# Layer 0's attention: one subtract on VectorE and one exponential of 512 columns in place of eight of 64

## The reference, cut to what matters

```python
scores = jnp.einsum('bhqd,bhkd->bhqk', Qm, Km) / jnp.sqrt(jnp.float32(Dh))
scores = jnp.where(attn_mask[:, None, :, :], scores, fill)
attn = jax.nn.softmax(scores, axis=-1)      # over 64 context tokens
A = jnp.einsum('bhqk,bhkd->bhqd', attn, Vm)
```

## Time and profile before

| what | value |
|---|---|
| median of 3 runs | 2477.66 us (2474.67 to 2482.07) |
| profiled execution, its own time | 2481.42 us |
| span of its profile | 2479.3 us |
| busy: TensorE, VectorE, ScalarE, GpSimd | 2241.2, 1453.5, 1420.2, 794.9 us |
| exponentials of the attentions (L1248) | 2048 instructions, 485.5 us of ScalarE |
| warm matmuls (L1031) | 1728 instructions, 450.1 us of TensorE |

### The profile page before, as it was taken

How to read it: one execution, slowest core, us unless ns; L and a number is a source line. 1 busy time by engine, 2 the same in 40 slices (tenths; PEclk the granted TensorE clock), 3 DMA queues, 4 the chain that set the end, 5 groups by cost and what they waited for, 6 DMA issues and landing times.

```text
span 2479.3 us, 42343 instructions
## 1 busy us (share of the span) xinstructions
PE 2241.2 (90%) x11319; PEld 1477.3 (60%) x11319; DVE 1453.5 (59%) x5504; ACT 1420.2 (57%) x5145; POOL 794.9 (32%) x870
## 2 busy tenths in 40 slices
PE   6979999999999989899999989898888988797987
PEld 3655756556565656566575747465655656575654
DVE  6554576676665657565676766575654646363621
ACT  2634658567484837474665757484664654665722
POOL 2121111201222222222133222223544444574655
PEclk9999999999999999999999999998999999888989
DMA  6030200100303030202021111204333332544323
GB/s 184 28 108 16 62 18 15 49 1 16 93 10 82 1 86 6 75 26 74 26 60 41 50 52 29 80 13 137 103 86 114 99 116 76 158 138 115 91 60 103
DMA packets 237206, 167.09 MB, mean 67 GB/s; under 512 B 97105, under 2 KB 230575, under 8 KB 236990
## 3 DMA queue, kind: packets, MB, share of 16 engines
q1 hardware_dynamic: 222654, 139.51, 20.1%
q0 software_dynamic: 14336, 25.28, 3.5%
HBM read 123.86 MB, written 53.40 MB: 71 GB/s over the span
## 4 chain that ended last, share of the span: by engine, by line
PE 51%; issue 14%; DVE 14%; ACT 8%; POOL 6%; SPq 4%; DMA 2%; DVEq 0%; POOLq 0%; another core or an unknown queue 0%; ACTq 0%
PE p L1055 8%; PE p L1014 6%; PE p L1031 6%; PE p L989 6%; PE p L952 4%; PE p L1003 4%; PE p L963 3%; PE p L946 3%; ACT l_scratch L1248 3%; PE pg L1023 2%; DVE ln_stats L1463 2%; PE p L1112 2%; SPq L788 2%; PE p L986 1%; DVE l_xres L1493 1%
## 5 line engine op out<-in xcount | busy, mean ns | idle before, releaser
L1248 ACT ACTIVATE l_scratch<-p,l_mx 128x64 f32<-128x64 f32 x2048 | 485.5, 324 | 37.2 <-DVE l_mx L1510 25.2
L1031 PE MATMUL p<-warm 128*128 128x512 bf16 x1728 | 450.1, 393 | 0.0
L1816 POOL TENSOR_TENSOR ln_rstd<-ln_ve,neghalf 128x4 f32<-128x4 f32 x96 | 98.4, 1025 | 731.6 <-DVE ln_ve L1472 730.4
L1023 PEld LDWEIGHTS pg<-slots,wcat 128*128 128x128 f32 x1024 | 175.2, 196 | 233.6 <-DVE slots L1764 161.1
L1014 PEld LDWEIGHTS p<-l_vg,l_scratch 128*128 128x128 f32 x2048 | 256.6, 194 | 60.8 <-ACT l_scratch L1256 33.3
L1031 PEld LDWEIGHTS p<-warm 128*128 128x128 bf16 x1728 | 177.5, 107 | 163.7 <-issue 35.3
L1014 PE MATMUL p<-l_vg,l_scratch 128*128 128x34 f32 x2048 | 262.3, 275 | 5.4 <-ACT l_scratch L1256 2.7
L1832 POOL TENSOR_TENSOR l_scratch<-l_scratch,gp 128x512 f32<-128x512 f32 x128 | 162.3, 1270 | 322.4 <-DVE l_sums L1515 321.4
L989 PE MATMUL p<-l_kbd,l_qT 128*128 128x512 f32 x512 | 262.8, 595 | 0.0
L1023 PE MATMUL pg<-slots,wcat 128*128 128x16 f32 x1024 | 178.3, 250 | 75.4 <-DVE slots L1764 54.9
L1510 DVE TENSOR_REDUCE l_mx<-p 128x8 f32<-128x512 f32 x256 | 176.4, 690 | 99.3 <-PE p L989 90.6
(11 more groups left out here) (302 smaller groups left out, 4120.1 us busy)
## 6 DMA issues: line engine op xcount, KB each, us to landing
xln<-xln_dram SPq DMA_DIRECT2D x40, 512.0 KB, 3.8
x_dram<-l_xres SPq DMA_DIRECT2D x32, 512.0 KB, 4.1
l_vg<-v_dram SPq DMA_DIRECT2D x30, 544.0 KB
l_kbd<-k_dram SPq DMA_DIRECT2D x512, 16.0 KB
xln_dram<-l_xnat SPq DMA_DIRECT2D x16, 512.0 KB, 3.0
l_xres<-x_dram SPq DMA_DIRECT2D x16, 512.0 KB
x_dram<-l_xnat SPq DMA_DIRECT2D x16, 512.0 KB
xin<-in_x SPq DMA_DIRECT2D x12, 512.0 KB, 3.7
```

The costliest lines, as they stand in the source:

```text
L1023: pe.matmul(pg[:, 0:B], wcat[:, :], slots[:, s % STEPS, :], start=True, stop=True).then_inc(l_pe, 1)
L1031: pe.matmul(banks[1][0] if layer > NC_ else px, warm[:, 0:P], warm[:, :], start=True, stop=True)
L1248: i = act.activation(w.ex[b % 2][:, NE * j + h, :], banks[lane][j][:, h * SK:(h + 1) * SK], ACT.Exp, scale=-1.0, bias=w.mx[:, u % 4, h:h + 1])
```

## The change

In layer 0 alone, the planner's four exp steps of a block become two: a new step `apart` on VectorE, and one exp step on ScalarE. `apart` waits for the minimum and for pturn u-4, subtracts each head's minimum from its 64 columns with one instruction of 512 columns (the minimum is read with a stride of zero along a head), and writes the difference from PSUM to `w.ex`. ScalarE then takes exp(-x) of those 512 columns in place, SBUF to SBUF, with no bias operand. Score u waits for `apart` of block u-2 and no longer for its exp. The semaphore `top` now tells that `apart` is done in layer 0 (in layer 1, as before, that the minimum is); the minimum in layer 0 and the sum in layer 1 share a renamed semaphore `reduced`.

```diff
     for u in range(2 * GB):
         steps += [
-            ("pe", "score", u, 1.1, [("qland", u % 2), ("neg", 0), ("exp", 4 * (u - 2) + 3)]),
+            ("pe", "score", u, 1.1, [("qland", u % 2), ("neg", 0), ("exp", 4 * (u - 2) + 3) if l else ("apart", u - 2)]),
             ("dve", "max", u, 0.65, [("score", u), ("exp", 4 * (u - 4) + 3)])]
-        steps += [("act", "exp", 4 * u + e, 0.45, [("max", u), ("pturn", u - 4)])
-                  for e in range(4)]
+        if l == 0:
+            steps += [("dve", "apart", u, 0.7, [("max", u), ("pturn", u - 4)]), ("act", "exp", 4 * u + 3, 0.62, [("apart", u)])]
+        else:
+            steps += [("act", "exp", 4 * u + e, 0.45, [("max", u), ("pturn", u - 4)]) for e in range(4)]
...
                 if family == "score":
                     if u < 2:
                         pe.wait_ge(t.lands, 4 * m + u + 1)
+                    elif layer == 0:
+                        pe.wait_ge(t.top, N - 1)
                     else:
                         pe.wait_ge(t.exped, N - 1)
...
                     (b, j), N = divmod(u, 2), 2 * GB * m + u
+                    if layer == 0:
+                        act.wait_ge(t.top, N + 1)
+                        part = w.ex[b % 2][:, NE * j:NE * j + NE, :]
+                        act.activation(part, part, ACT.Exp, scale=-1.0).then_inc(t.exped, 1)
+                        return
...
-                    dve.tensor_reduce(w.mx[:, u % 4, :], banks[l][j].rearrange("p (a k) -> p a k", a=NE), AX_X, ALU.min).then_inc(t.top, 1)
+                    dve.tensor_reduce(w.mx[:, u % 4, :], banks[l][j].rearrange("p (a k) -> p a k", a=NE), AX_X, ALU.min
+                                      ).then_inc(t.top if layer else t.reduced, 1)
+                elif family == "apart":
+                    dve.wait_ge(t.reduced, N + 1)
+                    if u >= 4:
+                        dve.wait_ge(t.turned, N - 3)
+                    dve.tensor_tensor(w.ex[b % 2][:, heads, :], banks[l][j].rearrange("p (a k) -> p a k", a=NE),
+                                      w.mx[:, u % 4, :].rearrange("p (a o) -> p a o", o=1).broadcast_to([P, NE, SK]),
+                                      ALU.subtract).then_inc(t.top, 1)
```

10 lines of the change are left out of this document (5 added, 5 removed).

## The result

The changed kernel takes 2469.04 us (median of 20 runs, 2456.92 to 2478.64), the kernel before 2477.57 us in the same comparison (20 runs). The ratio is 0.9962, 95% interval 0.9947 to 0.9977: faster by 8.5 to 9.4 us, where I had forecast 20. The time lies in the forecast range, but less than half of the gain came, and the first rival's 2475 us is nearer to it than my 2458.

What follows compares the result with a forecast made beforehand. It took TensorE to bound stage 0, the recurrent network stage 1, and ScalarE's exponentials part of stage 2's attention. Terms -1 + 5 - 24 = -20 us gave 2458 us from the median 2477.66; range 2447 to 2470, chance 0.50.

Steps and rivals of the forecast that it cites:

- the first rival: All attention: TensorE is the bound everywhere and filler was never in the way, so 2475 us; chance 0.18.
- Unit costs: Layer 0's blocks: new exponential 0.62 us, subtract 0.69; ScalarE's busy time falls about 164 us, VectorE's rises 88.
- Stage 0, -1: Stage 0's two bodies: TensorE is the bound with 1.5 us to give, so 1 us off for both.
- Stage 1, +5: Stage 1's two bodies: recurrent steps wait longer behind running long instructions, 0.08 us a step, 5 us slower for both.
- Stage 3, 3 us a body: Stage 3's bodies: relieved ScalarE lets attention shrink until TensorE is the bound, saving 3 us each.
- Stage 2, 3 us a body: Stage 2's bodies: exponentials bound part of attention; relieving ScalarE saves 3 us each, with VectorE staying below the bound.
- The slower one: Subtracts on VectorE delay stage 1's recurrence, 5.5 us a body, and stages 2 and 3, 0.5: 2493 us; chance 0.12.
- ScalarE as the bound everywhere: All attention windows: ScalarE, not TensorE, was at its bound, so stages 0, 2 and 3 shrink to 2417 us; chance 0.06.
- The Trainium skill's rule of weight loads: Weight-load busy time, not matmul time, measures TensorE, making ScalarE the bound in stage 0 as well: 2417 us.
- The fourth: As the forecast, plus norms and projections filling TensorE's gaps outside attention, 4 us more a body in four bodies: 2442 us; 0.14.

Runs made afterwards that it cites:

- half1: The changed kernel with stage 1's subtract and exponential each in two halves of 256 columns: 2478.82 us, ratio 0.9957 to the kernel before.
- No1: The changed kernel with stage 1 put back to eight exponentials of 64 columns: 2466.52 us, ratio 0.9928 to the kernel before.
- whole: Against the kernel before, layer 0 takes one 512-column exponential straight from PSUM, minimum taken but unused, no subtract: 2456.63 us, ratio 0.9885.
- the runs with the fill: The changed kernel, or it with stage 1 put back, plus 14 warm matmuls in stage 2's first body: ratios 0.9989 and 0.9895 to the kernel before.
- nomin: Against the kernel before, one 512-column exponential straight from PSUM in all four stages, neither minimum nor subtract in layer 0: 2439.20 us, ratio 0.9799.
- no1_fill: The changed kernel with stage 1 as before the change and 14 more warm matmuls in stage 2's first body: 2445.98 us, ratio 0.9895.

## Where the forecast was right and where it was wrong

- **Unit costs.** Right: 0.625 and 0.687 us a piece for 0.62 and 0.69. The busy times moved by 76 and 141 us for 88 and 164, by overlap for the most part.
- **Stage 0, -1.** Right in that the stage hardly moved (311.4 and 312.0 against 310.9 to 313.2), with TensorE at 35.00 of 35 us and the chain through it alone; a gain of 1 us can't be told from that spread.
- **Stage 1, +5.** The waits that I priced were about right, and the term was short by what I left out: +8 to +9. A step waits behind an instruction that runs, and half1 shows that its length counts. I had taken 32 steps with two crossings of 0.05 us behind subtracts, 3.2 us a body, and 3.6 were measured; behind exponentials I had 3.2 before and 2.6 after, and it was 3.8 and 1.2. Put together that is 1.0 us a body where I had 2.6. But each of the second body's 64 steps is 7.7 / 63 = 0.12 us longer, since in the new order they also fell behind minima, divisions and norms. For a new order I had no term, as if all else stood where it was. No1 has stage 1 back at 330.2 us. Its ratio of 0.9928 against 0.9962 prices more than stage 1: its ways into stage 2's repeats are 9.2 us shorter than in after.
- **Stage 3, 3 us a body.** Right: 3.4 in the repeated bodies. Some of it went into the ways between them (7.6 and 11.7 us before, 10.6 and 12.6 after, with a spread of 1 to 2 us in before itself), and the stage gave about 11 us for 12.
- **Stage 2, 3 us a body.** This is the step that failed. I wrote that "VectorE at 25.81 + 5.5 = 31 of 40 us stays below it" and let the subtract cost nothing. The long exponential alone brought 5.1 us a body, even more than I took. The subtract took back 3.7, so 1.4 were left. A busy share of 80% in the window was no reason for a price of nothing. It failed in a second way too: I took what the attentions give for what the body gives. They gave 3.9 us, but in the new order they start 6.7 us later, and only 4.1 of that came back behind them. Lane 1's chain, which goes through VectorE twice a block (minimum and sum) and through GpSimd, looks like the cause, and the traces don't bear it out: in the third body lane 1's sums reach over 46.9 us before, 39.0 in after and 36.9 in whole, so this chain is shorter after the change and at most 2 us longer by the subtract. Which wait makes the subtract cost 3.7 us stays open. To that came, in the first body, 6 to 7 us from the lower clock in 6 of 7 profiles, for which I had no term. The filler whose going I had counted as gain is what the runs with the fill put back, and with it TensorE had no second stretch at 1.2 GHz in that body.
- **The rivals.** TensorE at its bound everywhere (2475) is out: nomin goes on to 0.9799 with TensorE's work unchanged. The slower one is right in that the subtract costs as much as it says, 19 us over all stages against its 15, but in other places: 4 to 4.4 us a body of stage 1 for its 5.5, with the exponential in it, and 3.7 a body of stage 2 for its 0.5; and it left out the exponential's gain of 29. ScalarE as the bound everywhere (2417) is out as well, since 14 us less of ScalarE in stage 0's window left the stage as long as it was and its chain on TensorE. The Trainium skill's rule of weight loads, by which that rival went (Perfetto Trace Analysis, Identifying the Most-Contended Engine), isn't borne out there: TensorE is what the chain runs through, with 26.08 of 35 us of weight loads before, beside ScalarE's 31.53. The fourth, with 4 us more a body of stage 3 from outside attention, is out: the stage gave 11 us, and what stands outside its attentions grew by 2.7 us a body.
- **What stays open.** Stages 0 to 3 of the profiles make 1699.8 us before (mean of three) and 1695.6 after (mean of two), 4 of the 9 us measured. The rest would have to lie in stages 4 to 6, whose lengths differ by more than that between chips. The profiles are single executions, and the 20 runs on each side that give 9 us have no stages to compare.

The fastest kernel with the subtraction kept is no1_fill, the change without stage 1 and with the fill: 2445.98 us, ratio 0.9895. It beats both kernels, measured beside before and, on the same chip, the changed kernel (0.9967, 0.9949 to 0.9984).

## What to carry to other kernels

When work moves from a full engine to one that is 65% busy, price it twice: once alone, by a run that only adds it, and once as what stands ahead of the other chains on that engine. The question is not only whether the engine has room, but who waits behind the new instruction, and for a recurrence of short steps the length of one instruction counts. Where a planner makes the order, the new order is a term of its own: here the waits behind the new instructions were 1 us of the 8 that the recurrence of a body lost, and a gain inside the attentions was given back outside them. So measure the part that was changed and the parts around it apart. And filler that a better plan no longer has room for may have been holding the clock up.
